# Reordering the step of a fused ViT head, with five shared feed-forward pairs moved into its last steps

## The reference

```python
# x: (128 images, 64, 64, 3) -> 2048 tokens of width 128
xs = concat([x, *_shift4(x)])                       # image and its four shifts
y  = conv(xs, conv_w, stride 16) + conv_b           # patches
h  = layernorm(y) * gamma + beta;  h = h @ dense_w + dense_b
# attention over the 16 tokens of an image, 8 heads, a decay in place of a softmax
n  = layernorm(h); q, k, v = n@wq.T+bq, n@wk.T+bk, n@wv.T+bv
h  = h + silu(n@wg.T+bg) * ((q@k.T / sqrt(16) * decay) @ v)
# feed-forward with 64 experts, the best 2 for each token, and a shared part
n  = layernorm(h)
top, idx = top_k(sigmoid(n @ gate_w.T), 2)
routed = sum_k weight_k * w2[idx_k]^T (silu(n w1[idx_k]) * (n w3[idx_k]))
shared = silu(n @ sw1) * (n @ sw3) @ sw2
out = h + shared + routed
```

## Time and profile before

| | |
|---|---|
| time, median of 3 runs | 272.69 us (272.01 to 273.07) |
| the profiled execution: its time, its span | 270.12 us, 268.3 us |
| busy: PE, DVE, ACT, POOL | 183.7, 129.0, 86.6, 120.0 us |
| mean granted TensorE clock | 0.814 of full speed |
| head, up to the last send | 0 to 167 us |
| experts | 171.4 to 218 us |
| gathers, sums and stores | 221.8 to 268.3 us |

### The profile page before, as it was taken

The page is one execution under the profiler, slowest core; times in us unless marked ns, Lnnn a source line. Parts: engine busy times, 40 slices in busy tenths (PEclk is TensorE's granted clock), DMA queues, the critical chain, the costliest instruction groups (busy, mean ns, idle before and its releaser), DMA issues.

```text
span 268.3 us, 4422 instructions
## 1 busy us (share of the span) xinstructions
PE 183.7 (68%) x1385; PEld 128.3 (48%) x1385; DVE 129.0 (48%) x446; ACT 86.6 (32%) x228; POOL 120.0 (45%) x208
## 2 busy tenths in 40 slices
PE   0985688988888877987898531499999975552000
PEld 0432354655555545755566420399989953331000
DVE  2523154257776665457555627244645542223811
ACT  0030654344545564443554110145444411110000
POOL 3055222045655566455366675013232007777770
PEclk9999999579999997557555555599999999999555
DMA  7999999834665552244000001778843261222541
GB/s 268 372 374 374 416 400 429 319 145 176 174 175 168 162 127 76 49 88 100 10 22 20 22 20 38 194 191 245 275 145 113 68 170 43 51 59 53 147 98 29
DMA packets 29213, 42.95 MB, mean 160 GB/s; under 512 B 2752, under 2 KB 21376, under 8 KB 27904
## 3 DMA queue, kind: packets, MB, share of 16 engines
q1 hardware_dynamic: 26176, 35.27, 39.9%
q0 software_dynamic: 3008, 7.34, 9.4%
HBM read 24.45 MB, written 18.15 MB: 159 GB/s over the span
## 4 chain that ended last, share of the span: by engine, by line
PE 43%; POOL 24%; issue 13%; DMA 8%; DVE 5%; ACT 4%; SPq 2%; POOLq 1%; DVEq 0%
POOL X L1060 11%; PE bank L571 6%; POOL RS L1009 6%; PE scores L467 4%; DMA C<-cst 4%; PE bank L580 4%; PE bank L413 4%; PE bank L453 3%; PE scores L580 3%; ACT xrow L662 3%; PE bank L497 3%; PE bank L445 2%; POOL NM L1012 2%; PE bank L563 2%; PE bank L438 2%
## 5 line engine op out<-in xcount | busy, mean ns | idle before, releaser
L1033 POOL DMA_INDIRECT expert_rows<-xrow,slots x32 | 32.5, 1015 | 31.4 <-issue 30.3
L1060 POOL DMA_INDIRECT X<-expert_rows,slots x32 | 30.5, 955 | 23.0 <-DMA expert_rows<-ys 13.5
L413 PE MATMUL bank<-X,W 128*128 128x512 f32 x48 | 27.5, 684 | 7.4 <-DVE W L758 6.8
L673 ACT ACTIVATE qm<-bank,bqm,C 128x128 f32<-128x128 f32 x64 | 24.1, 456 | 10.0 <-PE bank L446 10.0
L922 DVE TENSOR_TENSOR hT<-bank,gs 64x512 f32<-64x512 f32 x17 | 11.8, 694 | 24.5 <-ACT gs L727 24.5
L1048 POOL DMA_DIRECT2D expert_rows<-ys x12 | 9.1, 760 | 32.2 <-DVE ys L935 32.2
L478 PE MATMUL scores<-vg,ST 64*64 64x16 f32 x512 | 21.8, 226 | 0.3 <-DVE ST L853 0.3
L478 PEld LDWEIGHTS scores<-vg,ST 64*64 64x64 f32 x512 | 20.2, 162 | 3.7 <-issue 2.6
L785 DVE BATCH_NORM_STATS2 stats<-bank 128x6 f32<-128x128 f32 x16 | 4.8, 299 | 33.6 <-PE bank L424 33.6
L435 PE MATMUL bank<-C,xrow 128*128 128x128 f32 x16 | 5.8, 366 | 20.3 <-ACT xrow L662 20.3
L662 ACT ACTIVATE xrow<-h,NM,RS 128x128 f32<-128x128 f32 x16 | 7.9, 493 | 36.3 <-POOL NM L1012 36.3
(11 more groups left out here) (131 smaller groups left out, 382.6 us busy)
## 6 DMA issues: line engine op xcount, KB each, us to landing
expert_rows<-EW SPq DMA_DIRECT2D x10, 1024.0 KB, 19.4
X<-xp SPq DMA_DIRECT2D x12, 512.0 KB, 14.1
xb<-expert_rows SPq DMA_DIRECT2D x16, 256.0 KB, 3.9
expert_rows<-ys POOLq DMA_DIRECT2D x12, 256.0 KB, 3.2
EW<-w SPq DMA_DIRECT2D x4, 512.0 KB, 5.4
EW<-wp SPq DMA_DIRECT2D x3, 640.0 KB, 6.2
XE<-xe SPq DMA_DIRECT2D x4, 384.0 KB, 15.7
expert_rows<-ys SPq DMA_DIRECT2D x4, 256.0 KB, 2.5
```

The costliest lines, as they stand in the source:

```text
L413: mm = nc.tensor.matmul(CONV[:, :], w, x, start=(j == 0), stop=(j == NCH + 1))
L673: nc.scalar.activation(qm[:, t % 2, m], QK[:, 0:P], ACT.Identity, bias=bqm[:, m:m + 1], scale=head[:, m:m + 1])
L1033: pool.indirect_dma_start(buf, bass.IndirectOffsetOnAxis(ap=slots[:, k, t:t + 1], axis=0), xrow[:, t % XR], None).then_inc(sent[t % XR], 16)
L1060: pool.indirect_dma_start(pr[:, t, k], None, buf, bass.IndirectOffsetOnAxis(ap=slots[:, k, t:t + 1], axis=0)).then_inc(pr_in[t // TS], 16)
```

## The change

On each engine the calls of a head step stand in another order. On PE the embedding of tile i+1 moves from the step's end to its middle, `turn` moves behind `scores`, the second patch product moves in between `turn` and `logits`. On DVE `decay_scores` moves from the end of a step to the start of the next, `embedded` moves up, `attended` is split in `gated` (the product with the gate) and the rest, and `y_stats` of the next tile moves in from the next step. On ACT `evac_y` moves ahead of `evac_qk`. On POOL the two sends of a tile are issued one step later. Besides, the first EARLY = 5 of the 8 pairs of the shared feed-forward leave the kernel's end: pair p goes up in step 16 + p and down in the step after.

```diff
+        EARLY = LAST - NT
@@ PE @@
             embed(0)
             for i in range(LAST):
+                conv_step(i, 0)
+                if i > NT:
+                    shared_down(i - 1 - NT)
                 if 0 <= i - 3 < NT:
                     attend(i - 3)
-                conv_step(i, 0)
+                if i >= NT:
+                    shared_up(i - NT)
+                if i + 1 < NT:
+                    embed(i + 1)
                 if 0 <= i - 5 < NT:
                     places(i - 5)
+                if 0 <= i - 2 < NT:
+                    scores(i - 2)
                 if FIRST2 <= i <= LAST2:
                     turn(i)
-                if 0 <= i - 2 < NT:
-                    scores(i - 2)
+                conv_step(i, 1)
                 if 0 <= i - 4 < NT:
                     logits(i - 4)
                 if 0 <= i - 1 < NT:
                     project(i - 1)
-                conv_step(i, 1)
-                if i + 1 < NT:
-                    embed(i + 1)
+            shared_down(EARLY - 1)
@@ ACT @@
                     tanhs(i - 4)
+                if i % TG == 2 and i // TG + 1 < NG:
+                    evac_y(i // TG + 1)
                 if 0 <= i - 1 < NT:
                     evac_qk(i - 1)
                     evac_vg(i - 1)
-                if i % TG == 2 and i // TG + 1 < NG:
-                    evac_y(i // TG + 1)
+                if i >= NT:
+                    shared_gate(i - NT)
@@ DVE @@
-            def attended(t):
+            def gated(t):
 
                 dve.wait_ge(av_ps, t + 1)
                 dve.wait_ge(g_ready, t + 1)
...
                 ins.then_inc(av_read, 1)
+
+            def attended(t):
+
                 dve.wait_ge(av_read, t + 1)
...
+            y_stats(0)
             for i in range(LAST):
-                if i < NT:
-                    y_stats(i)
+                if 0 <= i - 3 < NT:
+                    decay_scores(i - 3)
                 if 0 <= i - 5 < NT:
                     choose(i - 5)
+                if i < NT:
+                    embedded(i)
+                if 0 <= i - 3 < NT:
+                    gated(i - 3)
+                if i > NT:
+                    shared_add(i - 1 - NT)
+                if i + 1 < NT:
+                    y_stats(i + 1)
                 if 0 <= i - 3 < NT:
                     attended(i - 3)
                 if 0 <= i - 5 < NT:
                     place(i - 5)
-                if i < NT:
-                    embedded(i)
-                if 0 <= i - 2 < NT:
-                    decay_scores(i - 2)
+                if i >= NT:
+                    shared_hidden(i - NT)
+            shared_add(EARLY - 1)
@@ POOL @@
                     accumulate(i - 5)
+                if 0 <= i - 6 < NT:
                     for k in range(TOPK):
-                        send(i - 5, k)
+                        send(i - 6, k)
+            for k in range(TOPK):
+                send(NT - 1, k)
@@ the shared pairs at the end, on PE, ACT and DVE @@
-            for p in range(NS):
+            for p in range(EARLY, NS):
```

## The result

| | us |
|---|---|
| before, median of 4 runs | 272.88 (272.01 to 275.69) |
| changed, median of 4 runs | 257.81 (253.65 to 263.99) |
| ratio | 0.932, 95% interval 0.919 to 0.946 |
| predicted | 268.7 (263.5 to 273.5) |

The change makes the kernel 7% faster, 11 us more than predicted and outside the range. The changed kernel's executions spread over 10 us, and the longer ones show the lower granted clocks (0.832 for 253.65 us, 0.783 for 263.99). The profiled one took 259.68 us, with a span of 257.9. These are its rows on the page: the engines' busy time, and the granted clock in 40 slices of 6.4 us.

What follows compares the result with a forecast made beforehand. The prediction took a ring through POOL, ACT, PE and DVE to bound the head and POOL's gathers the last stage. The head gains 15.0 us, the drain takes back 11.0: 272.69 - 4.0 = 268.7 us, range 263.5 to 273.5.

Steps and rivals of the forecast that it cites:

- the half-clock steps: Head from step 11, without patch products: clock at half, 7.7 us a step in place of 8.3.
- marker 14: Start of the q product in step 14, forecast at 111.1 us after steps 12 to 14 at 7.7 each.
- marker 16: Start of the q product in step 16, where the drain begins: forecast at 127.0 us, head 15.0 early.
- the rival in which the clock stays full: Full clock throughout from step 11, steps at most 5.6 us in place of 7.7: 249 us, chance 0.03.
- The full-speed steps: Head steps at full clock, before step 11: 7.10 us shortens to 6.13, with PE as the bound.
- The wait for `gated`: PE's short wait ahead of the scores in a full-speed step: 0.13 us, added to 6.00 of PE work.
- Marker 10: Start of the q product in step 10: forecast at 81.8 us, 12.3 early, after six steps of 6.13.
- Marker 4: Start of the q product in step 4: forecast at 45.0 us in place of 48.12.
- The rival that DVE takes over in these steps: DVE's chain replaces PE's as bound of full-speed steps: 6.9 us a step, 274.9 us in all, chance 0.12.
- three falls: Clock falls in the full-speed steps, an alternative in the costlier-drain rival: 271.5 us, no tellable change, chance 0.17.
- The drain: From the q product of step 16 to the last send: 35.0 us in place of 24.0, taking back 11.0.
- The end: After the last send: five pairs of 3.36 us leave it and gain nothing, since the gathers cover them.

Runs made afterwards that it cites:

- again_2: The changed kernel, unaltered, measured a second further time: 254.32 to 265.01 us in six runs, ratio to before 0.946.
- again: The changed kernel, unaltered, measured once more: 253.16 to 278.81 us in four runs.
- no_pairs: The changed kernel with all eight shared pairs back at the end, order and sends as changed: 243.84 us.
- pairs_only: The kernel before, its step order and sends kept, with the five shared pairs moved into the drain: 284.74 us against 273.43 for before.
- order_alone: The changed kernel's order with all eight pairs at the end and the sends in the step of their place: 287.73 us, ratio to before 1.005.
- send_same: The changed kernel, five early pairs kept, with each tile's two sends back in the step of its place: 286.85 us.
- send_late: The kernel before, all eight pairs at the end, with only the sends going out one step later: 280.62 us, ratio to before 0.975.
- slow_mid: no_pairs, with DVE also zeroing an unread buffer six times in each of steps 7 to 10: 267.02 us.
- no_pairs_2: The changed kernel with all eight pairs at the end, measured once more: 246.01 us, ratio to before 0.893.

## Why the prediction was wrong

**The step that failed is the half-clock steps**: "Is it at half clock? I take it that it is". I let the clock fall in step 11 in every execution. In the profile after it fell behind marker 14. Steps 12 to 14 took 5.1 to 5.3 us in place of 7.7, and marker 14 came at 103.7 instead of 111.1. Of the 10.9 us by which the median was missed, 6.4 are in the span (264.3 by my sum, 257.9 measured): marker 16 came 6.9 early (120.1 for 127.0), and the drain gave 1.0 of that back. The other 4.4 are the two offsets: this execution is 1.87 above its median, and I had put the 2.57 of before on top. The four executions of before lay close together (272.01 to 275.69), and I took that for a property of the kernel; in a later group its eleven went from 270.61 to 283.4.

My reason was that a step which waits less also works less. The runs show that the falling clock is a matter of the execution, at 88.1, 103.7 and 116.9 us in three profiles of one program. The case that I forecast happens: that is the profile with a span of 270.0. It is not the likeliest: of the 14 executions of the changed kernel, three took 268 us or more. Between it and the rival in which the clock stays full, with its chance of 0.03, I had no case in which it falls later, and two of the three profiles are that case. The Trainium skill asks to keep long idle gaps out of PE's work (TensorE: Matmul & The Clock Gate, section Why this matters for your kernels). That only such gaps take the clock back, as I read it in the prediction, is half right here: the clock held through step 15 of again_2 with a wait of 1.10 us, and fell in again with nothing longer than 0.53 in the two steps before it. The same page's section "A second HAM failure mode: psum-queue depth-cycling" tells of a kernel in which short waits between groups of products take the clock to and fro. The fall in again, without a long wait, agrees with that; but there the clock did not go to and fro, it stayed at half until 177 us.

**The full-speed steps**: the mechanism was right. The step fell to PE's bound, 5.80 us for a forecast of 6.13. The term that was too large is PE's work, recorded as 6.00 us in the old step and 5.58 in the new one for the same products. The wait for `gated` ahead of the scores is 0.21, not 0.13, and 0.42 in the steps without patch products. Marker 10 came at 83.1 for 81.8, since steps 7 and 8 took 3.0 us more than two of 5.79. Some 2 of these are a fall of the clock, half from 62.8 to 66.2, which I had priced at 1.5 and left out. The other 1.0 is a term that my sum does not have: in again and again_2, whose clock held there, step 7 still took 7.0 and 6.8 us. POOL's first two sends, late and ahead of the next deviation in its queue, hold up `embedded` there, and PE waits for it:

```profile
61.10 0.30 PE L424 MATMUL bank<-C,yT 128*128 128x128 f32 x1 [0.90 <-DVE h L851]
```

Marker 4 was at 45.3 for 45.0, in part by luck: step 2, which I had left unchanged, took 0.7 us less, and marker 1 came 1.1 later. The rival that DVE takes over in these steps did not happen. In the steps without patch products DVE is busy for 4.54 of 5.10 us, and from 83.3 to 103.7 us the profile records no wait of it. One slip in the rivals: three falls at my price of 1.5 us give 273.2 and not 271.5.

**The half-clock steps' size** was near in the profile after: 7.5 us for 7.1 in step 15 and 8.9 for 8.8 in step 16. It was not in again, where the clock fell where I had put it: steps 12 to 16 took 8.6 to 9.0 us, and marker 16 came at 132.6 for 127.0 (last section).

**The drain**: 36.0 us for 35.0, and its reason, PE's in-order queue behind `shared_down` and `shared_up`, is shown by no_pairs and pairs_only (13.4 and 11.8 us). Its steps were within 0.5 us: the gates at 123.25, 133.36, 142.22 and 148.63 are 10.1, 8.9 and 6.4 apart for 9.6, 8.6 and 6.2. That the sends of tile 14 would cost some 2 us without the pairs fits no_pairs, where four sends back to back end the drain; no run took them away alone.

**The end**: right. Pairs that leave it give nothing while the gathers cover them; the last section has the moment when they did not.

**The later sends** I had costed only as a bound on POOL's step. order_alone shows that they are the condition of everything else: with the sends in their old place the new order gains nothing, and with the pairs (send_same) it loses 13 us.

## What to carry to other kernels

A reordering has a condition, and it is often in another engine's queue: look for what the new order makes late (here the row numbers) and who is queued behind the one that waits for it. Work that is hidden behind transfers is free where it is; moved to a stage of short chained steps it costs most of its own length (here 2.3 to 3.2 us for a pair of 3.36), for its chain crosses three engines and the steps queue behind it. And where a stage runs near the point at which the granted clock falls, forecast both levels with their chances and their whole spread: one program here had 253.2 to 278.8 us.

## What the hardware did that I had not expected

**At half clock, the same product was done after two different times.** In the profile of again, DVE's `gated` waits 3.18 us for an `attend` that has the same recorded start-to-end as in no_pairs, where it waits 1.82. First `attend` and `gated` in again:

```profile
107.99 1.89 PE L479 MATMUL scores<-vg,ST 64*64 64x16 f32 x32
...
111.31 0.59 DVE L817 TENSOR_TENSOR go<-scores,vg 64x128 f32<-64x128 f32 x2 [3.18 <-PE scores L479]
```

Then the same one of no_pairs, whose `attend` starts at 103.58:

```profile
105.52 0.59 DVE L810 TENSOR_TENSOR go<-scores,vg 64x128 f32<-64x128 f32 x2 [1.82 <-PE scores L479]
```

From the start of `attend` it is 3.32 us in one and 1.94 in the other, at a granted clock of 0.50 in both. The steps are 8.9 us long in again and 7.6 in no_pairs; this later result is about the whole difference. What causes it is open.

**The last shared pairs can be late.** In the group of runs in which before took 286.40 us, the three kernels with eight pairs at the end that were profiled (send_late, order_alone, slow_mid) took 115 us from the last send, in place of 102. The waits of ACT in the profile of slow_mid show where:

```profile
227.70 0.38 ACT L696 ACTIVATE shg<-bank 128x256 f32<-128x256 f32 x1 [7.50 <-remote]
244.50 0.38 ACT L696 ACTIVATE shg<-bank 128x256 f32<-128x256 f32 x1 [16.42 <-remote]
```

PE had started the second product for these gates at 223.19 and 235.56, beside the gathers; the gates start 4.5 and 8.9 us later, where 0.6 was usual. The changed kernel, in the same group, has only three pairs there, all done before, and ended 101.4 us after its last send. A later group on the same chip had before at 273.57 us, and no_pairs_2 no such wait. So it belongs to the moment and not to the program or the chip, and while it lasts, the early pairs save an estimated 13 us at the end (115 less 102), about what they cost in the drain. I did not find what it is.
